# A fused attention and expert block: token statistics by BN_STATS on VectorE, and a new order at four borders

## What is computed

```python
x = x + conv_attention(ln_c(x))          # ln_c: mean and variance over the 64 channels of each pixel
# conv_attention:
qkv = einsum('bchw,oc->bohw', x, w_qkv)                       # 192 channels: 24 groups of 8
dw  = conv 5x5, depthwise;  pw = einsum per group of 8 channels, w_pw
ms  = concat([qkv, pw])                                       # 16 heads of q, k, v with 8 channels each
kv  = relu(k)^T [v, 1];  out = relu(q) kv;  out = out[:-1] / (out[-1] + 1e-15)
out = einsum(out, w_proj) * inv + (beta - mean * inv)         # batch norm at inference
t = tokens(x)                                                 # 2048 tokens of 64
l = ln_t(t) @ Wg + bg;  top 2 of 8, softmax over the two
t = t + sum_e weight_e * (gelu(ln_t(t) @ W1[e] + b1[e]) @ W2[e] + b2[e])
```

## Time and profile before

| | us |
|---|---|
| median of 3 runs | 131.77 (131.23 to 132.6) |
| profiled execution | 131.66 |
| its span | 129.8 |
| TensorE busy | 123.1 |
| VectorE / ScalarE / POOL busy | 81.9 / 85.8 / 27.7 |

### The profile page before, as it was taken

The page is one execution under the profiler, slowest core; times in us unless marked ns, Lnnn a source line. Parts: engine busy times, 40 slices in busy tenths (PEclk is TensorE's granted clock), DMA queues, the critical chain, the costliest instruction groups (busy, mean ns, idle before and its releaser), DMA issues.

```text
span 129.8 us, 2655 instructions
## 1 busy us (share of the span) xinstructions
PE 123.1 (95%) x922; PEld 98.2 (76%) x922; DVE 81.9 (63%) x242; ACT 85.8 (66%) x201; POOL 27.7 (21%) x29
## 2 busy tenths in 40 slices
PE   6999899999999999979999999989999999999980
PEld 7499799999998899867786785746666767666650
DVE  0418999999984987885586047991727245090551
ACT  3347999999972947258989497096491947829100
POOL 3004999800000000240460004000000000000681
PEclk9999999999999999999999999999999999999998
DMA  4889200000000000000000057009508600194001
GB/s 117 233 196 255 59 3 0 0 5 0 0 3 0 5 0 0 0 5 0 0 0 0 5 130 194 6 11 230 135 5 206 158 0 0 23 241 110 0 0 43
DMA packets 5062, 7.72 MB, mean 59 GB/s; under 512 B 1298, under 2 KB 3642, under 8 KB 5050
## 3 DMA queue, kind: packets, MB, share of 16 engines
q1 hardware_dynamic: 4672, 7.34, 22.8%
q10 hardware_dynamic: 378, 0.22, 0.6%
HBM read 6.97 MB, written 0.59 MB: 58 GB/s over the span
## 4 chain that ended last, share of the span: by engine, by line
PE 86%; DVE 3%; DMA 3%; POOL 2%; ACT 2%; issue 1%; POOLq 1%; DVEq 0%; ACTq 0%
PE PS L887 57%; PE PS L1096 19%; PE PS L988 3%; DMA CST<-in_consts_dram 3%; POOL XP L388 2%; DVE MS L608 2%; PE PS L994 1%; PE PS L1025 1%; PE PS L1011 1%; PE PS L947 1%; PE PS L1052 1%; PE PS L1055 1%; POOLq L79 1%; ACT KR L437 1%; ACT MS L515 1%
## 5 line engine op out<-in xcount | busy, mean ns | idle before, releaser
L515 ACT ACTIVATE MS<-PS,B 128x512 f32<-128x512 f32 x48 | 29.2, 681 | 12.0 <-PE PS L887 12.0
L807 DVE SCALAR_TENSOR_TENSOR SQ<-PS,B,BAND 128x256 f32<-128x256 f32 x32 | 14.4, 480 | 22.6 <-PE PS L1096 17.8
L887 PE MATMUL PS<-XS,W1H 128*128 128x512 f32 x64 | 27.0, 422 | 1.1 <-ACT XS L499 0.7
L887 PE MATMUL PS<-QP,BAND 128*128 128x120 f32 (+2 forms) x240 | 27.0, 275 | 0.2 <-DVE QP L639 0.2
L887 PEld LDWEIGHTS PS<-QP,BAND 128*128 128x128 f32 x240 | 26.9, 192 | 0.4 <-issue 0.4
L887 PE MATMUL PS<-XS,W1L 128*128 128x512 f32 x64 | 25.2, 395 | 0.0
L1096 PE MATMUL PS<-MS,W 128*64 128x256 f32 x192 | 22.3, 383 | 0.0
L1096 PEld LDWEIGHTS PS<-MS,W 128*64 128x64 f32 x192 | 13.2, 137 | 8.5 <-ACT MS L515 1.1
L887 PEld LDWEIGHTS PS<-XS,W1H 128*128 128x128 f32 x64 | 12.0, 187 | 7.5 <-issue 3.3
L426 ACT ACTIVATE BAND<-RS,PW 128x80 f32<-128x80 f32 x64 | 17.2, 429 | 0.0
L388 POOL TENSOR_TENSOR XP<-XP,SQ 128x256 f32<-128x256 f32 x7 | 5.1, 727 | 42.5 <-DVE SQ L807 41.7
(11 more groups left out here) (114 smaller groups left out, 163.9 us busy)
## 6 DMA issues: line engine op xcount, KB each, us to landing
BAND<-spread_dram SPq DMA_DIRECT2D x16, 256.0 KB, 4.7
W<-in_w_dram SPq DMA_DIRECT2D x3, 512.0 KB, 6.2
X<-in_x_dram SPq DMA_DIRECT2D x2, 256.0 KB, 3.4
out_dram<-XP SPq DMA_DIRECT2D x4, 128.0 KB, 2.3
VEC<-in_vectors_dram SPq DMA_DIRECT2D x1, 132.0 KB, 3.7
SELF<-in_select_dram ACTq DMA_DIRECT2D x1, 100.8 KB
WQ<-in_w_qkv_dram SPq DMA_DIRECT2D x2, 48.0 KB, 3.5
PW<-in_w_pw_dram SPq DMA_DIRECT2D x1, 96.0 KB, 3.0
```

Source lines behind the costliest of these rows:

```text
L515: act.activation(hidden(n), PS[:, h_bank(n), :], ACT.Gelu, bias=B1[:, k:k + 1]).then_inc(gelu_done, 1)
L807: dve.scalar_tensor_tensor(out=WY[:, e % 2, :], in0=PS[:, bank, at:end], scalar=B2[:, e:e + 1], in1=WB[:, s % 2, e, :], op0=ALU.add, op1=A ...
L887: return pe.matmul(PS[0:parts, bank, cols[0]:cols[1]], lhsT, rhs, start=start, stop=stop)
```

## The change

The statistics are no longer taken by matmuls. VectorE and ScalarE bring x to token order (three quarters and one quarter of each half), TensorE transposes it into PSUM with an identity (turn_tokens), and VectorE runs one BN_STATS for each of 16 groups of 64 channels; four small operations combine its two half-sets to a variance. Root and correction are as before. The identity (IDT) and the centring matrix (CEN) are made by POOL with affine_select and no longer come by DMA, and CST shrinks to 26 columns. There are 8 zero tiles and one more between the halves. ScalarE copies WQC and all four quarters of RS.

The last head of the convolution goes v, k, q, each part into a bank of its own and moved by itself (move_last).

XN and ScalarE's high are gone: VectorE writes the rounded high part straight away, and the low part with 4 scalar_tensor_tensor of 64 elements. residual is split into centre and whole, and the lists of VectorE, ScalarE and TensorE around the end of the attention are written in a new order; the hidden banks' ring of two serves 6 products instead of 4.

tokens(s) moves to where a run of first layers begins, with read_tokens ahead of that run's gelus. The weights of pair 0 come back in three parts of 2, 2 and 4 experts.

```diff
         CHAIN_BANK = (6, 0, 2, 4)
-        H_FEW, H_MANY, FEW = (6, 7), (0, 1, 6, 7), 4
-        Y_BANKS, LAST_Y_BANKS = (2, 3, 4), (2, 3, 4, 5, 0, 1, 6, 7)
+        H_FEW, H_MANY, FEW = (6, 7), (0, 1, 6, 7), 6
+        Y_BANKS, LAST_Y_BANKS = (2, 3, 4), (2, 3, 4, 5, 6, 7, 0, 1)
         TOKEN_BANK = 5
...
+                parts = ((0, 1), (1, 2), (2, 4)) if s == 0 else ((0, 2), (2, 4))
+                for first, last in parts:
                     for b in range(2):
-                        rows = slice(E * b + QUAD * quad, E * b + QUAD * quad + QUAD)
...
             pool.memset(WARM[:, :], 0.0).then_inc(warm_set, 1)
+            pool.memset(IDT[:, :], 1.0).then_inc(ones_made, 1)
+            pool.wait_ge(ones_made, 1)
+            pool.affine_select(out=IDT[:, :], in_=IDT[:, :], pattern=[[1, 128]], compare_op=ALU.is_equal, fill=0.0,
+                               base=0, channel_multiplier=-1).then_inc(ident_made, 1)
+            pool.memset(CEN[:, :], 0.0).then_inc(ones_made, 1)
+            pool.wait_ge(ones_made, 2)
+            for h in range(2):
+                same = slice(C * h, C * h + C)
+                pool.memset(CEN[same, same], -1.0 / C).then_inc(ones_made, 1)
...
+            act.dma_start(WDF[:, :], w_dw).then_inc(dw_in, 16)
             act.dma_start(SELF[:, :], select).then_inc(sel_in, 16)
             act.preload_act_table(ACT.Sqrt)
-            act.wait_ge(sel_in, 32)
+            act.wait_ge(x_in[0], 16)
+            act.activation(*in_token_order(0, 1), ACT.Copy).then_inc(xp_s, 1)
+            act.wait_ge(x_in[1], 16)
+            act.activation(*in_token_order(1, 1), ACT.Copy).then_inc(xp_s, 1)
+            act.wait_ge(sel_in, 16)
             act.activation(SEL[:, :], SELF[:, :], ACT.Copy).then_inc(sel_high, 1)
-            for k in range(2):
...
+            act.wait_ge(wqc_ready, 1)
+            act.activation(WQC[:, :], PS[:, WQC_BANK, 0:QKV], ACT.Copy).then_inc(wqc_copied, 1)
             copy_rs(0)
+            copy_rs(1)
             act.wait_ge(var_ready, 1)
             act.wait_ge(pads_set, 5)
-            act.activation(DEV1[:, :], PS[:, VAR_BANK, 0:16], ACT.Sqrt, bias=EPS1[:, :]).then_inc(dev1_ready, 1)
-            copy_rs(1)
+            act.activation(DEV1[:, :], VAR1[:, 3, :], ACT.Sqrt, bias=EPS1[:, :]).then_inc(dev1_ready, 1)
             copy_rs(2)
...
-                act.wait_ge(xn_ready, s + 1)
-                if s >= 2:
-                    act.wait_ge(a_filled[s - 2], A_XT)
-                act.activation(XHL[:, s % 2, :, 0, :].bitcast(F32R), XN[:, s % 2], ACT.Copy).then_inc(hi_ready, 1)
             def copy_xs(s):
...
             square_xc(2)
             copy_attt(3)
+            gelu(0, 1)
+            copy_xs(1)
             gelu(0, 2)
+            square_xc(3)
             gelu(0, 3)
-            high(2)
-            square_xc(3)
+            copy_xs(2)
             gelu(0, 4)
-            copy_xs(2)
             gelu(0, 5)
             gelu(0, 6)
-            high(3)
             read_tokens(0)
             copy_xs(3)
             gelu(0, 7)
-            for e in range(4):
...
                 gelu(1, e)
             for s in (2, 3):
+                read_tokens(s)
                 for e in range(E):
                     gelu(s, e)
-                    if e == 1:
-                        read_tokens(s)
         @block.vector
         def _(dve):
...
+            def order_tokens(k):
                 dve.wait_ge(x_in[k], 16)
-                dve.tensor_copy(pair_tokens(XP, k), by_pixel(X[:, 512 * k:512 * k + 512])).then_inc(xp_ready, 1)
-            dve.wait_ge(sel_in, 32)
+                dve.tensor_copy(*in_token_order(k, 0)).then_inc(xp_v, 1)
+            def statistics(k):
+                for jp in (2 * k, 2 * k + 1):
+                    dve.wait_ge(tokens_up, jp + 1)
+                    for n in range(4):
+                        i = dve.bn_stats(STATS[:, 4 * jp + n, :], PS[:, STATS_BANKS[jp], C * n:C * n + C])
+                i.then_inc(stats_done, 1)
...
                               ALU.subtract).then_inc(wd_split, 1)
-            dve.wait_ge(wqc_ready, 1)
-            dve.tensor_copy(WQC[:, :], PS[:, WQC_BANK, 0:QKV]).then_inc(wqc_copied, 1)
+            order_tokens(1)
+            statistics(0)
+            statistics(1)
+            dve.wait_ge(stats_done, 2)
+            dve.tensor_tensor(VAR1[:, 0, :], STATS[:, :, 1], STATS[:, :, 4], ALU.subtract)
+            link(dve.tensor_tensor(VAR1[:, 1, :], STATS[:, :, 2], STATS[:, :, 5], ALU.add))
...
+                dve.transpose(head(8 + h), of).then_inc(conv_moved, 1)
+            def move_last(q):
+                dve.wait_ge(conv_ready, 10 - q)
+                dve.transpose(head(15)[:, q], PS[:, LAST_BANKS[q], 0:128].rearrange("p (y b) -> p b y", b=B))\
                     .then_inc(conv_moved, 1)
...
             def low(s):
-                dve.wait_ge(xn_ready, s + 1)
                 dve.wait_ge(hi_ready, s + 1)
-                dve.tensor_tensor(XHL[:, s % 2, :, 1, :].bitcast(F32R), XN[:, s % 2], XHL[:, s % 2, :, 0, :],
-                                  ALU.subtract).then_inc(xh_ready, 1)
+                for t in range(TILES):
+                    i = dve.scalar_tensor_tensor(out=XHL[:, s % 2, t, 1, :].bitcast(F32R), in0=XC2[:, s % 2, t],
+                                                 scalar=SM[:, s, 1, t:t + 1], in1=XHL[:, s % 2, t, 0, :],
+                                                 op0=ALU.mult, op1=ALU.subtract)
+                i.then_inc(xh_ready, 1)
             def read_gates(part):
...
-            residual(0)
+            centre(0)
+            whole(0)
+            variance(0)
             attend(2)
-            variance(0)
             read_kv(3)
-            residual(1)
             scale(0)
+            low(0)
+            centre(1)
+            whole(1)
+            attend(3)
             variance(1)
-            low(0)
-            residual(2)
+            centre(2)
+            whole(2)
             scale(1)
             low(1)
-            attend(3)
+            variance(2)
+            centre(3)
+            whole(3)
+            scale(2)
+            low(2)
             read_gates(0)
-            variance(2)
             gaps(0)
-            scale(2)
-            residual(3)
...
+            def warm_up(count):
+                for _ in range(count):
+                    mm(WARM_BANK, (0, 128), WARM[:, :], WARM[:, :], True, True)
+            warm_up(WARM_UPS)
+            def turn_tokens(k):
+                pe.wait_ge(xp_v, k + 1)
                 for j in range(4 * k, 4 * k + 4):
-                    i = mm(VAR_BANK, (2 * j, 2 * j + 2), SQ[:, 128 * j:128 * j + 128], ONES, True, True)
-                if k == 1:
-                    i.then_inc(var_ready, 1)
+                    if j % 4 == 3:
+                        pe.wait_ge(xp_s, k + 1)
+                    i = pe.transpose(PS[:, STATS_BANKS[j // 2], 128 * (j % 2):128 * (j % 2) + 128],
+                                     pixel(j, slice(0, 128)), IDT[:, :])
+                    if j % 2 == 1:
+                        i.then_inc(tokens_up, 1)
...
             rs(1)
             rs(2)
+            pe.wait_ge(wqc_copied, 1)
             rs(3)
-            pe.wait_ge(wqc_copied, 1)
-            pe.wait_ge(xp_ready, 2)
+            pe.wait_ge(stats_done, 2)
             qkv(0)
-            pe.wait_ge(r1_ready, 1)
             qkv(1)
-            pe.wait_ge(rs_copied, 2)
+            pe.wait_ge(rs_copied, 3)
             qkv(2)
-            pe.wait_ge(rs_copied, 3)
-            pe.wait_ge(rs_copied_v, 1)
+            pe.wait_ge(rs_copied, 4)
             qkv(3)
...
+                    if q == 2 or h == 7:
                         i.then_inc(conv_ready, 1)
-            i.then_inc(conv_ready, 1)
...
-            xt(0)
             first_layer(0, 0)
+            attt(3)
+            first_layer(0, 1)
+            proj(3)
             xt(1)
-            first_layer(0, 1)
-            attt(3)
+            first_layer(0, 2)
             gate(0)
-            first_layer(0, 2)
             first_layer(0, 3)
-            proj(3)
+            xt(2)
             first_layer(0, 4)
             first_layer(0, 5)
...
-            first_layer(1, 4)
             tokens(1)
-            for e in range(5, E):
+            for e in range(QUAD, E):
                 first_layer(1, e)
             for e in range(QUAD):
                 second_layer(1, e)
             for s in (2, 3):
-                first_layer(s, 0)
-                first_layer(s, 1)
                 tokens(s)
-                first_layer(s, 2)
-                first_layer(s, 3)
+                for e in range(QUAD):
```

More of the change, by code:

```diff
@@ L87, in build @@
         X = sb("X", [128, 4 * N])
+        CEN = sb("CEN", [128, 128])
+        IDT = sb("IDT", [128, 128])
         CST = sb("CST", [128, C_END])
@@ L157, in build @@
         XC2 = late(2, TILES, C)
-        XN = late(2, TILES, C)
         XHL = late(2, TILES, 2, C)
@@ L172, in build @@
```

(26 more changed lines are left out.)

171 lines of the change are left out of this document (78 added, 93 removed).

## The result

The changed kernel takes **127.28 us** (4 runs, 127.22 to 127.42) against 132.19 of the kernel before (4 runs, 131.23 to 132.75): ratio 0.9638, 95% interval 0.9573 to 0.9702. Forecast were 128.6, with a range of 127.6 to 130.6. The direction was right, the size too small: the time lies 0.3 us under the range. The profiled execution took 127.27, its span is 125.6. Some executions of a kernel take longer than its others, up to 136.8 us for the kernel before and most of them at a lower granted clock; ratios and intervals leave out those over 1.5% above the fastest, the medians of the experiments count them in.

The account below looks back on a forecast made before the run. TensorE, busy 123.1 of 129.8 us, bounds the kernel; 1.6 + 0.28 + 0.7 + 0.45 + 0.1 = 3.1 us off 131.66 gives 128.55, with 0.11 to the median 128.6, range 127.6 to 130.6.

Parts of the forecast that it names:

- the fourth term: Tokens at run borders and pair 0's weights: 0.45 us saved by moving tokens(1), 0.1 by the weights.
- The weights in three parts: Pair 0's second layers: the first quarter of the weights comes sooner, removing a TensorE wait of 0.1 us.
- The moves for pairs 2 and 3: Tokens of pairs 2 and 3 moved ahead of their first layers: meet no hole, costed at nothing.
- it has no other wait between 15 and 120 us: TensorE between 15 and 120 us: no further waits, so it can use the summed saving of 3.1 us.
- The first term: Start: statistics by VectorE's bn_stats instead of matmuls let scaling start 1.6 us earlier, and all behind it.
- Rival A: Start: bn_stats at 0.25 us instead of 0.158 lengthen VectorE's chain by 1.5 us; 130.1 us, chance 0.17.
- The warm-ups at nothing: Start: the 8 warm-up tiles, two more than before, end before half 0's transposes could help VectorE; cost nothing.
- rival C: Start: POOL's identity comes late, then idle TensorE's clock falls; 4.9 us lost there, 135 us in all, chance 0.05.
- The last head: End of the convolution: order v, k, q with separate moves removes TensorE's idle ahead of kv(0), 0.28 us saved.
- The middle: Attention to experts: high and low on VectorE, xt(0) ahead of proj(2); first layer 0.8 earlier, net 0.7 us.
- Rival B: Attention to experts: proj(3) waits 1 us or more behind ScalarE's queue, saving becomes -0.1; 129.4 us, chance 0.11.
- Rival D: Whole kernel: no gain reaches the end, x lands later or holes reappear behind; 131.2 us, chance 0.05.

Follow-up runs that it names:

- t_back: Changed kernel with tokens(1), tokens(2), tokens(3) and ScalarE's read_tokens back in their old places: 128.57 us, against 127.59 for the changed kernel beside it.
- b_tok1: Kernel before with only tokens(1) moved ahead of first_layer(1, 4): 131.29 us against 131.75, ratio 0.9936.
- wb_two: Changed kernel with pair 0's weights in two parts as before: 127.62 us, against 127.59 for the changed kernel beside it.
- bn_twice: Changed kernel with each of the 16 bn_stats run twice, the first into a spare tile: 129.49 us, ratio 0.9833 to the kernel before.
- warm_6: Changed kernel with 6 warm-up tiles instead of 8 and none between the halves: median 129.4 us, ratio 0.9690 to the kernel before.
- high_act: Changed kernel with the high part rounded on ScalarE again, new order kept: 129.87 us, ratio 0.9838 to the kernel before.
- head_back: Changed kernel with the convolution's last head again k, v, q, k and v moved together: 127.82 us, ratio 0.9694 to the kernel before.

## Why the prediction was right, and where it was wrong

**The step that failed is the fourth term**, tokens and weights. It read "TensorE waits 0.45 until 85.89" and booked 0.45. That column counts from the modelled end of the record before, and a record is 0.40 long where the step is 0.234. Counted by starts, the hole is 85.89 - 85.04 - 0.234 = 0.62. From there to the second layers the 8 matmuls take 2.28 (85.89 to 88.17), the last 8 of the changed kernel 1.96 (82.33 to 84.29): 0.32 more, since TensorE, once behind ScalarE's gelus, stays paced by them. And the tokens, put into a running row of first layers, cost one more long step of 0.32 instead of 0.23, 0.09. By the two chains the sum is 1.02, which is what t_back lost (1.03 in the trace up to there; 0.98 in time, all three pairs together) and b_tok1 gained in its trace. The right reading was the length of the whole stretch, 5.30 us, less its work, 4.28. The weights in three parts were sized at 0.1 from the 0.12 of "issue" in the chain; the chain had 3.94 us for 32 records of second layers that take 3.60 elsewhere. That 0.3 is in the traces of before and wb_two, and not in the medians of wb_two. The moves for pairs 2 and 3 were put at nothing and gave 0.12: 4.35 and 4.33 before, 4.28 each after. And "it has no other wait between 15 and 120 us", said of TensorE in the sum, came from the same column.

**The first term** came out at 1.50 for 1.6, by two errors that cancel by luck. BN_STATS was taken at 0.158 and took 0.136 (0.35 us less in all); the three-quarter copy at 0.45 by size and took 0.81, so that the statistics started at 5.82 and not at 5.4. They ended at 8.00, forecast 7.93. Rival A needed 0.25 each and is out; bn_twice shows that its mechanism, VectorE's chain without slack, was right. POOL's operations took 0.29 (under 0.5 foreseen).

**The warm-ups at nothing**: they cost nothing to run, as forecast, but their use was reckoned as time only, and in warm_6's trace what they bring is an earlier clock. Of rival C its second half is seen there in small: TensorE idle at the start for 1.08 us, then matmuls at the lower level until about 8.3, and not through the whole start. Its first half is not seen: the identity was done at 1.50. The Trainium skill, "TensorE: Matmul & The Clock Gate", Part 1, has an idle TensorE fall back to half rate. The profiled execution of high_act is in line with that (a hole with 0.98 us idle, then a granted clock of 0.50). That of b_tok1 is not: its clock fell to 0.50 with TensorE at work since 3.94, so idleness is not the only thing that brings it down.

**The last head** is right by place and size (0.28; head_back 0.28).

**The middle** is right by its net, 0.75 for 0.7, and the first expert layer came at 55.55, 2.9 us earlier, for 2.7. Its two halves missed in opposite directions, so that the net is partly luck: from kv(0) to the first expert layer the gain was 1.12 (16.13 before, 15.01 after) for 0.8, and behind it 0.37 was given back (10.41 and 10.78) for 0.1. The waits that were named came: from the first expert layer to proj(3) TensorE takes 2.88 for 2.31 of work (8 steps of 0.234 and attt(3)'s 0.44), 0.57 for the 0.5 forecast, and the step ahead of 62.36, where it waits for the reading of the gates, is 0.40, 0.17 for the 0.2 forecast. Rival B, a middle that does not pay, is out by the net. VectorE's four instructions of the low part in its timeline:

```profile
53.27 0.87 DVE L756 SCALAR_TENSOR_TENSOR BAND<-BAND,SM 128x64 fp32r<-128x64 f32 x4
```

0.2 us each, the upper end of what was taken. By the half rate of the Trainium skill, "Vector Engine (DVE) Microarchitecture Reference", section 7, some 0.3 us more are the estimate for the four; 0.07 to 0.27 came, and no run here separates that from the cost of four small instructions. It was hidden.

**Rival D** is out: the gain grows from each place of the table to the next. By the list of waits TensorE's longest, after that for its first tile, is 0.3 us.

**Open**: 0.23 between the last addition and the end (the output's DMAs land in a median of 1.7 us instead of 2.3) and 0.19 outside the span. Nothing in the change aims at them and no experiment separated them. The 0.09 up to the last addition are no such rest: they are the 0.12 of tokens(2) and tokens(3), less 0.03 elsewhere.

## What to carry to other kernels

Size a stall by the length of the whole stretch less its work at the unhindered step, not by the idle column: where records overlap, it hides part of the stall and all of the slower pace behind it (here 0.45 shown, 1.02 lost). Ask of every filler on TensorE what happens to the clock without it, not only whether somebody waits. And a split that takes work off an engine must be timed by its shape: here three quarters of a copy took longer than the whole.

## What the hardware showed that I had not expected

- VectorE's copy of fp32 into token order takes 0.60 us for 512 elements per partition (4 of 4 pixels) and 0.80 to 0.81 for 384 (3 of 4), with ScalarE copying beside it and without; 128 elements take 0.25.
- BN_STATS on 64 fp32 elements in PSUM takes 2.18 us for 16 back to back, 0.136 each; 16 more on the path cost 2.09, 0.13 each (bn_twice).
- In high_act's trace a hole with 0.98 us idle in the middle of a busy stream was followed by about 3 us at a granted clock of 0.50, and the slow stretch cost more than the hole. Three of six executions had no such stretch, and in b_tok1's trace the clock stood at 0.50 from about 10 to 16 us with no hole ahead.
- The granted clock reads full in the first microseconds, while 128-column matmuls have records of 0.42 us there and of 0.27 later: at the start, go by the records.
- affine_select on 128x128 takes POOL 0.29 us, from 1.21 on, with no pause to load anything before it (its MODIFY_POOL_CONFIG stand at 1.1).
